# A mixing layer: the branch's part added on TensorE and ScalarE during the scaling turns, and six scaled additions a tile on VectorE instead of ten

## What is computed

```python
H_res = sinkhorn_log(x_norm @ W_res.T + base)         # 4x4 a row, 50 iterations
H_pre, H_post = softmax(x_norm @ W_pre.T + ..), softmax(x_norm @ W_post.T + ..)
H_res = (1 - g) * I + g * H_res
x_pre = einsum('btnc,btn->btc', x_streams, H_pre)
y = x_pre @ W_branch                                    # the branch
x_mixed = einsum('btij,btjc->btic', H_res, x_streams)
return x_mixed + einsum('btc,btn->btnc', y, H_post)
```

## Time and profile before

| | |
|---|---|
| time, median of 3 runs | 2952.16 us (2950.13 to 2953.05) |
| the profiled execution | 2949.29 us |
| its span | 2947.6 us |
| granted TensorE clock, mean | 0.94 of full speed |
| PE busy | 2588.3 us (88%), 15056 instructions |
| DVE busy | 1821.9 us (62%), 4485 instructions |
| ACT busy | 1082.8 us (37%), 2317 instructions |

### The profile page before, as it was taken

How to read it: one execution, slowest core, us unless ns; L and a number is a source line. 1 busy time by engine, 2 the same in 40 slices (tenths; PEclk the granted TensorE clock), 3 DMA queues, 4 the chain that set the end, 5 groups by cost and what they waited for, 6 DMA issues and landing times. The chain is left out here.

```text
span 2947.6 us, 50657 instructions
## 1 busy us (share of the span) xinstructions
PE 2588.3 (88%) x15056; PEld 1807.8 (61%) x15056; DVE 1821.9 (62%) x4485; ACT 1082.8 (37%) x2317; POOL 1123.7 (38%) x801
## 2 busy tenths in 40 slices
PE   7999997999998899553759999978999987996999
PEld 6665644765553688542647555536665644885887
DVE  5677775567774433788766766764677773215443
ACT  2345554154555211442511545542355554002000
POOL 7456553555664000000044655536456552002110
PEclk9999998999999899666979999989999998998999
DMA  4323312432320521000134322223232313434111
GB/s 163 102 84 84 95 49 68 147 92 66 102 69 30 180 71 43 0 0 7 80 128 135 86 83 85 79 73 110 77 96 78 103 42 138 141 121 150 65 64 44
DMA packets 121079, 252.95 MB, mean 86 GB/s; under 512 B 12720, under 2 KB 39728, under 8 KB 120880
## 3 DMA queue, kind: packets, MB, share of 16 engines
q1 hardware_dynamic: 120912, 251.03, 26.7%
HBM read 166.57 MB, written 84.41 MB: 85 GB/s over the span
## 5 line engine op out<-in xcount | busy, mean ns | idle before, releaser
L617 ACT ACTIVATE a_prob<-a_pst 128x512 f32<-128x512 f32 (+3 forms) x1536 | 660.9, 493 | 572.2 <-PE a_pst L898 566.4
L710 DVE CUSTOM_DVE_ANT_0 a_psh<-a_psh,a_edge 128x128 f32<-128x128 f32 (+3 forms) x1024 | 480.1, 516 | 198.0 <-PE a_psh L851 170.6
L851 PE MATMUL a_psh<-a_kst,a_qst 127*128 127x512 f32 (+3 forms) x1536 | 485.3, 364 | 26.3 <-DVE a_mx L710 14.4
L898 PE MATMUL a_pst<-a_qst,a_kst 128*128 128x512 f32 (+2 forms) x1536 | 487.2, 372 | 23.1 <-DMA a_qst<-rowmax 18.6
L517 POOL TENSOR_TENSOR a_prob<-a_prob 128x2048 f32<-128x2048 f32 (+1 forms) x96 | 405.6, 4225 | 242.5 <-PE a_ppv L914 242.5
L851 PEld LDWEIGHTS a_psh<-a_kst,a_qst 127*128 127x128 f32 x1536 | 272.4, 189 | 240.2 <-DVE a_mx L713 92.7
L713 DVE TENSOR_REDUCE a_mx<-a_psh 128x1 f32<-128x512 f32 x512 | 329.3, 685 | 127.3 <-PE a_psh L851 126.2
L898 PEld LDWEIGHTS a_pst<-a_qst,a_kst 128*128 128x128 f32 x1536 | 287.5, 194 | 163.9 <-ACT a_prob L617 103.5
L914 PE MATMUL a_ppv<-a_prob,a_vg 128*32 128x512 f32 (+3 forms) x3072 | 319.2, 502 | 0.0
L502 POOL TENSOR_SCALAR_AFFINE_SELECT a_prob<-a_prob 128x512 f32<-128x512 f32 x256 | 161.9, 639 | 188.1 <-ACT a_prob L617 187.9
L927 PE MATMUL a_pden<-a_prob,a_ones 128*32 128x512 f32 (+3 forms) x2304 | 220.1, 475 | 14.1 <-POOL a_prob L517 14.1
(11 more groups left out here) (227 smaller groups left out, 4164.1 us busy)
## 6 DMA issues: line engine op xcount, KB each, us to landing
a_qst<-q SPq DMA_DIRECT2D x192, 256.0 KB, 4.5
a_wraw<-in_wqkv SPq DMA_DIRECT2D x52, 512.0 KB, 4.3
q<-a_stg_hi SPq DMA_DIRECT2D x64, 256.0 KB, 2.1
q<-a_stg_lo SPq DMA_DIRECT2D x64, 256.0 KB, 2.4
a_kst<-kT SPq DMA_DIRECT2D x96, 128.0 KB, 2.6
oT<-a_oT SPq DMA_DIRECT2D x32, 256.0 KB, 2.4
oT<-a_vT SPq DMA_DIRECT2D x32, 256.0 KB, 2.9
h_oraw<-oT SPq DMA_DIRECT2D x16, 512.0 KB, 4.0
```

The costliest lines, as they stand in the source:

```text
L617: act.activation(prob[k % len(prob)][:, h, off:], pst[:, (k * GH + h) % 3, off:], ACT.Exp, scale=scale).then_inc(s["exp_done"], 1)
L710: part = dve.tensor_tensor_reduce(scores, scores, edge[:, BANK - n:], 1.0, 2 * MASKED, ALU.add, ALU.max, mx_hq[kc][:, h, qt:qt + 1])
L851: mm = pe.matmul(psh[:, at, i * n:(i + 1) * n], qst[par][0:P - 1, h, qt * P:(qt + 1) * P], kst[par][0:P - 1, kc * BANK:kc * BANK + n], sta ...
L898: pe.matmul(pst[:, (k * GH + h) % 3, off:], kst[par][:, ki * P:(ki + 1) * P], qst[par][:, h, qc * BANK + off:(qc + 1) * BANK], start=True, ...
```

## The change

Four things are altered, all within `mixing_layer`.

- In the scaling turns each tile gets its branch part: ScalarE writes four more diagonals with H_post (semaphore `dq`), TensorE forms in `h_pout` the sum of the identity times the old stream and the H_post diagonal times y, for all four streams (eight products, `add_branch`, semaphore `xy`), and ScalarE copies the 128x1024 result back over `h_x` (`copy_x`, semaphore `xc`). These run one turn late: turn t adds the branch of tile t-1.
- The normalised tile is written once, into `z_all`, four tiles at a time: tiles 0 to 3 ahead of the turns, then 4 to 7, 8 to 11 and 12 to 15 inside turns 1, 5 and 9, as a loop of ScalarE. y is kept in two small buffers.
- The turns are written out (`for t in range(NT)`), where they were a loop on the engine.
- In the last phase no product and no addition concerns y. TensorE makes streams 0 and 1 with four products each and half of stream 2 (its terms 0 and 1, in the PSUM buffer `h_pz`); ScalarE still writes ten diagonals a tile. VectorE makes stream 3 and the other half of stream 2 with six scaled additions, in groups of two, two, one and one with a drain between them, then adds `h_pout` as before, and `h_pz` in a second, 128x256 addition.

```diff
-    PR0, PT0, YR0, Y0, MI0 = 1, 1, 1, 1, 2
-    HALF = NS // 2
+    PR0, PT0, YR0, MI0 = 1, 1, 1, 2
+    ON_PE = [(i, n) for i in range(2) for n in range(NS)] + [(2, 0), (2, 1)]
+    ON_DVE = (((3, 0), (2, 2)), ((3, 1), (2, 3)), ((3, 2),), ((3, 3),))
+    NP = len(ON_PE)
...
-            with act.Fori(0, NT) as t:
-                act.wait_ge(s["pre_ready"], t + 1)
-                act.activation(z[0][:, :], tile(x, t), ACT.Identity, bias=nmr[:, ds(t, 1)],
-                               scale=rstd[:, ds(t, 1)]).then_inc(s["z2"], 1)
+            def normalised(first):
+                with act.Fori(first, first + 4) as t:
+                    act.activation(tile(z_all, t), tile(x, t), ACT.Identity, bias=nmr[:, ds(t, 1)],
+                                   scale=rstd[:, ds(t, 1)]).then_inc(s["z2"], 1)
+            def pre_diagonals(t):
                 for n in range(NS):
-                    act.activation(dg[0][:, n, :], ident[:, :], ACT.Copy, scale=pp[:, ds(t, 1), 0, n])\
+                    act.activation(dg[0][:, n, :], ident[:, :], ACT.Copy, scale=pp[:, t, 0, n:n + 1])\
                         .then_inc(s["dp"], 1)
-                act.activation(tile(z_all, t), tile(x, t), ACT.Identity, bias=nmr[:, ds(t, 1)],
-                               scale=rstd[:, ds(t, 1)])
+            def copy_x(t):
+                act.wait_ge(s["xy"], t + 1)
+                act.activation(x[:, t, :], pout[:, :, :].rearrange("p a n -> p (a n)"), ACT.Copy).then_inc(s["xc"], 1)
+            def branch(t):
                 act.wait_ge(s["pre_ready"], PR0 + t + 1)
                 act.wait_ge(s["y_ready"], t + 1)
                 act.activation(preT[:, :, :], ppre[:, 0:C].rearrange("p (k n) -> p k n", n=P), ACT.Copy)\
                     .then_inc(s["preT"], 1)
+                if t % 4 == 1 and t + 3 < NT:
+                    normalised(t + 3)
+                if t + 1 < NT:
+                    pre_diagonals(t + 1)
+                if t:
+                    copy_x(t - 1)
+                for n in range(NS):
+                    act.activation(dg[0][:, NS + n, :], ident[:, :], ACT.Copy, scale=pp[:, t, 1, n:n + 1])\
+                        .then_inc(s["dq"], 1)
                 act.wait_ge(s["y_ready"], YR0 + t + 1)
-                act.activation(tile(y_all, t), py[:, 0:C], ACT.Copy).then_inc(s["y"], 1)
+                act.activation(y[t % 2], py[:, 0:C], ACT.Copy).then_inc(s["y"], 1)
+            normalised(0)
+            pre_diagonals(0)
+            for t in range(NT):
+                branch(t)
+            copy_x(NT - 1)
...
-                    for i in range(HALF):
-                        for n in range(NS):
-                            act.activation(dg[par][:, i * (NS + 1) + n, :], ident[:, :], ACT.Copy,
-                                           scale=m[:, ds(t, 1), i * NS + n]).then_inc(s["dm"], 1)
-                        act.activation(dg[par][:, i * (NS + 1) + NS, :], ident[:, :], ACT.Copy,
-                                       scale=pp[:, ds(t, 1), 1, i]).then_inc(s["dm"], 1)
+                    for at, (i, n) in enumerate(ON_PE):
+                        act.activation(dg[par][:, at, :], ident[:, :], ACT.Copy,
+                                       scale=m[:, ds(t, 1), i * NS + n]).then_inc(s["dm"], 1)
...
-            dve.wait_ge(s["y"], Y0 + NT)
+            dve.wait_ge(s["xc"], NT)
             with dve.Fori(0, NT // 2) as j:
                 for par in range(2):
                     t = j * 2 + par
-                    for n in range(NS):
-                        zn = z_all[:, ds(t, 1), n * C:(n + 1) * C].rearrange("p o n -> p (o n)")
-                        for i in range(HALF, NS):
-                            dve.scalar_tensor_tensor(stream(t, i), zn, m[:, ds(t, 1), i * NS + n], stream(t, i),
-                                                     ALU.mult, ALU.add)
-                        dve.drain()
-                    for i in range(HALF, NS):
-                        dve.scalar_tensor_tensor(stream(t, i), tile(y_all, t), pp[:, ds(t, 1), 1, i], stream(t, i),
-                                                 ALU.mult, ALU.add)
+                    for at, terms in enumerate(ON_DVE):
+                        if at:
+                            dve.drain()
+                        for i, n in terms:
+                            dve.scalar_tensor_tensor(stream(x, t, i), stream(z_all, t, n), m[:, ds(t, 1), i * NS + n],
+                                                     stream(x, t, i), ALU.mult, ALU.add)
                     dve.wait_ge(s["mix"], MI0 + t + 1)
-                    cols = x[:, ds(t, 1), 0:HALF * C].rearrange("p o n -> p (o n)")
-                    dve.tensor_tensor(cols, cols, pout[:, par, 0:HALF * C], ALU.add)
+                    cols = x[:, ds(t, 1), 0:2 * C].rearrange("p o n -> p (o n)")
+                    dve.tensor_tensor(cols, cols, pout[:, par, :], ALU.add)
+                    dve.tensor_tensor(stream(x, t, 2), stream(x, t, 2), pz[:, par, 0:C], ALU.add)
...
+            def add_branch(t):
+                pe.wait_ge(s["y"], t + 1)
+                pe.wait_ge(s["dq"], NS * t + NS)
+                for n in range(NS):
+                    cols = pout[:, n // 2, n % 2 * C:n % 2 * C + C]
+                    pe.matmul(cols, ident[:, :], x[:, t, n * C:(n + 1) * C], start=True, stop=False, skip_group_check=True)
+                    mm = pe.matmul(cols, dg[0][:, NS + n, :], y[t % 2], start=False, stop=True,
+                                   skip_group_check=True)
+                mm.then_inc(s["xy"], 1)
+            def branch(t, first):
                 pe.wait_ge(s["z2"], t + 1)
                 pe.wait_ge(s["preT"], t + 1)
                 pe.wait_ge(s["dp"], NS * t + NS)
                 for c in range(C // P):
                     for n in range(NS):
-                        mm = pe.matmul(ppre[:, c * P:(c + 1) * P], z[0][:, n * C + c * P:n * C + (c + 1) * P],
+                        mm = pe.matmul(ppre[:, c * P:(c + 1) * P],
+                                       z_all[:, t, n * C + c * P:n * C + (c + 1) * P],
                                        dg[0][:, n, :], start=(n == 0), stop=(n == NS - 1))
                 mm.then_inc(s["pre_ready"], 1)
-                pe.wait_ge(s["y"], t + 1)
+                if t > 1:
+                    pe.wait_ge(s["xc"], t - 1)
+                if not first:
+                    add_branch(t - 1)
                 pe.wait_ge(s["preT"], PT0 + t + 1)
                 for k in range(C // P):
                     mm = pe.matmul(py[:, 0:C], preT[:, k, :], wb[:, k, :], start=(k == 0), stop=(k == C // P - 1))
                 mm.then_inc(s["y_ready"], 1)
-            pe.wait_ge(s["y"], Y0 + NT)
+            for t in range(NT):
+                branch(t, t == 0)
+            pe.wait_ge(s["xc"], NT - 1)
+            add_branch(NT - 1)
+            pe.wait_ge(s["xc"], NT)
             with pe.Fori(0, NT // 2) as j:
                 for par in range(2):
                     t = j * 2 + par
                     pe.wait_ge(s["mixed"], t + 1)
-                    for i in range(HALF):
-                        for n in range(NS + 1):
-                            if n == 0:
-                                pe.wait_ge(s["dm"], (t * HALF + i) * (NS + 1) + NS + 1)
-                            rhs = z_all[:, ds(t, 1), n * C:(n + 1) * C].rearrange("p o n -> p (o n)") if n < NS \
-                                else tile(y_all, t)
-                            mm = pe.matmul(pout[:, par, i * C:(i + 1) * C], dg[par][:, i * (NS + 1) + n, :], rhs,
-                                           start=(n == 0), stop=(n == NS), skip_group_check=True)
+                    for at, (i, n) in enumerate(ON_PE):
+                        if n == 0:
+                            pe.wait_ge(s["dm"], t * NP + min(at + NS, NP))
+                        out = pout[:, par, i * C:(i + 1) * C] if i < 2 else pz[:, par, 0:C]
+                        mm = pe.matmul(out, dg[par][:, at, :], stream(z_all, t, n), start=(n == 0),
+                                       stop=(i, n + 1) not in ON_PE, skip_group_check=True)
                     mm.then_inc(s["mix"], 1)
```

More of the change, by code:

```diff
@@ L1140, in mixing_layer @@
         "stats", "rstd", "rms_in", "rms", "z", "zT_ready", "zT", "logit", "read", "gate", "e_in", "e_out",
-        "pp", "z2", "dp", "pre_ready", "preT", "y_ready", "y", "h_res", "dm", "mix", "mixed", "stored")}
+        "pp", "z2", "dp", "pre_ready", "preT", "y_ready", "y", "dq", "xy", "xc", "h_res", "dm", "mix", "mixed", "stored")}
     w_loaded, o_loaded, x_loaded = [s[f"wl{k}"] for k in range(KC)], (s["ol0"], s["ol1"]), (s["x0"], s["x1"])
     M0, L0, S0, ZR0, ZT0, LG0, RD0, MX0, DMA0 = 4, 2, 2, 4, 2, 2, 2, 2, 16
-    PR0, PT0, YR0, Y0, MI0 = 1, 1, 1, 1, 2
-    HALF = NS // 2
+    PR0, PT0, YR0, MI0 = 1, 1, 1, 2
+    ON_PE = [(i, n) for i in range(2) for n in range(NS)] + [(2, 0), (2, 1)]
+    ON_DVE = (((3, 0), (2, 2)), ((3, 1), (2, 3)), ((3, 2),), ((3, 3),))
+    NP = len(ON_PE)
```

(15 more changed lines are left out.)

## The result

The changed kernel takes 2913.31 us, the median of four runs (2911.69 to 2916.31), against 2951.14 us before: a ratio of 0.9876 with a 95% interval of 0.9862 to 0.9891, or 37.8 us less. The forecast was 2928 with a range of 2923 to 2941. The direction was right, the size too small: 24 us were forecast. The profiled execution has a span of 2912.1 us, 35.5 less than the 2947.6 before.

What follows compares the result with a forecast made beforehand. Sinkhorn, the first tile, then VectorE's fifteen tiles were taken to bound the mixing layer; -0.29 (first tile) + 0.35 (second addition) - 15 x 1.61 = -24.1 us, so 2952.16 became 2928, range 2923 to 2941.

Steps and rivals of the forecast that it cites:

- What bounds the stage: Mixing layer: Sinkhorn on VectorE, the first tile on TensorE, then fifteen tiles on VectorE set its end; turns had 42 us spare.
- The tile: Last phase on VectorE: each tile 1.61 us shorter, from 6.42 to 4.81 us, over 15 tiles.
- The chain: Last phase, VectorE's scaled additions up to a tile's 128x512 addition: 3.21 us instead of 5.17, 1.96 less.
- the unseen addition: Last phase, VectorE's new 128x256 addition of `h_pz`, not in the old trace: 0.35 us a tile, between 0.26 and 0.60.
- over 5 was the sign: Last phase: if right, VectorE waits for TensorE in the first tile alone, now over 5 us.
- The first tile: Start of last phase: TensorE's first product waits for four diagonals instead of five, so it starts 0.29 us earlier.
- The turns: Scaling turns beside Sinkhorn: 8.2 us each at full clock, ending at 1356, 29 us before `h_res`, at no cost.
- the 3.79 of the `h_ppre` sums: Scaling turns on TensorE: the sums for `h_ppre` were put at 3.79 us at most within a turn.
- A: Scaling turns: TensorE stays at the lower clock, turns of 12.7 us outlast Sinkhorn, kernel 14 us slower, 2966; chance 0.06.
- B: Last phase: TensorE becomes the bound below clock 0.90; at 0.75 a tile takes 5.76, total 2942; chance 0.10.
- C: Scaling turns: turns of about 11 us end 12 us late and halve the gain, about 2946; chance 0.04.
- None of the three is late next: Last phase: TensorE, ScalarE's diagonals and the tile's store all keep up with 4.81 us a tile; TensorE is nearest.

## Why the prediction was wrong in size

- **What bounds the stage**: right. Sinkhorn, the first tile, then VectorE's tiles, before and after.
- **The tile**: right in mechanism, and 0.10 us a tile too long: forecast 4.81, measured 4.71. The chain was met (3.20 for 3.21) and the unseen addition too (0.33 for 0.35). The addition is 0.02 of it; most of the rest, 0.07, is the idle time between tiles, which I carried over: 0.37 and 0.79 in turn before, 0.38 and 0.63 now. The runs show that the second of these, at the loop's top, moves with the code (0.93 and 1.19 with only the branch moved). In all fifteen tiles give 25.7 and not 24.2 us. VectorE's wait in the first tile is 4.5 us, where over 5 was the sign.
- **The first tile**: -0.29 forecast, -1.1 measured. The 7.3 us of products were 6.4, because the clock rose sooner: from 1390 to 1393 it is 1.00, where the kernel before has 0.75 from 1391 to 1394. That is chance: the kernel before with drains that came later than this tile has 7.99, the unchanged kernel 8.95, the changed one 7.81 and 8.45 in its two runs.
- **The turns**: no cost, as forecast, but the size was off: 8.2 us a turn forecast, 6.3 measured, end at 1323.6 for 1356. The step that failed is the 3.79 of the `h_ppre` sums, taken from rows at the lower clock while the rest of the turn was priced at the full one. With 1.95 in its place the prediction's own sum gives 6.7 a turn, by ScalarE's way. The clock did rise: 0.90 in the stretch, 0.96 up to the turns' end. The cover is 60 us, and 55 us more work in it were free.
- **Rivals**: A was priced right (each us beyond Sinkhorn's end is paid in full) and did not occur; its ground, a clock that stays at the 0.70 of the old turns, is not there: the new turns have 0.96. The swing of the clock with short pauses that the Trainium skill describes ("TensorE: Matmul & The Clock Gate", section "A second HAM failure mode: psum-queue depth-cycling") does not show in them. They hardly test it, as TensorE works 104 of their 118.6 us. B did not occur: VectorE waited for TensorE once. C's doubt, what written-out code costs in the turns, came to nothing: neither ScalarE nor TensorE has an idle piece over 0.8 us in them without a releaser.
- **The step that made it wrong**: that the sum ends with the mixing layer. "None of the three is late next" spoke of this stage alone, and the later stages stand in the sum at nothing, without a reason given. Their code is the same, but its place is not: a pass of the last phase's loop holds 16 instructions fewer in VectorE's program (62 before, 46 now, counted in the traces), and behind the two jumps of the next stage's loop that saves 4.1 + 3.8 = 7.9 us. The stage as a whole is 9.4 us shorter; the other 1.5 are within what the same kernel varies by. Putting 16 instructions back makes the two stretches 7.8 us longer and the median 2923.8, just inside the range. The mixing layer itself gave 27.8 us for the 24.1 forecast: 1.5 in the fifteen tiles, 0.8 in the first and 1.5 ahead of Sinkhorn. The trace of before held the hint: two stages of the same code, 846.3 and 858.0 us from first to last scan.

What stays open: why the second load comes 4 us behind the first and not at once, and what moves the stage by some us away from the two jumps, in the changed kernel against itself too. The change also writes out loops of TensorE and ScalarE and so moves the later code of both; no run moved that back, and only what lies behind the two jumps is shown to come from VectorE's.

## What to carry to other kernels

Price a change also by the instructions that it takes out of or puts into an engine's program, since all later code on that engine moves with them, as VectorE's did here; when two stages run the same code, compare their lengths first, and if they differ, look for idle pieces named "issue" at the loop's top. Before a change is judged by a few us, a run with some do-nothing instructions in a spot where the engine is idle tells how much of the figure is the place of the code; look at the stretches where the pauses stand, as whole stages of one trace vary by some us. And work beside a long serial stretch on another engine is free up to its end and costs in full beyond it, so its duration has to be worked out at the clock that the new load itself brings about.

## What the runs showed of the hardware

- At jumps back to the top of the attention's loop VectorE stands idle for about 2 us (1.9 to 2.4 in all runs) with nothing to wait for, and goes on about 2 us after a load of 8192 bytes began on an instruction queue. Where the instructions lie 16 further on, in the kernel before and with 16 drains, there is one piece of about 6 us instead (6.14 and 5.75; 5.78 and 5.77). That the edge between two loads falls right behind the loop's top there is the explanation that fits, argued from the loads' times.
- 112 drains behind the last tile lengthen the layer's end by 2.2 us in the changed kernel and by 1.7 in the old one; 16 and 64 lengthen it by 1.2 each.
- Eight 32-bit products of 128 columns take 1.95 us at a granted clock of 1.00 and 3.79 at 0.50 (the sums of `h_ppre`).
- Work on TensorE and ScalarE beside Sinkhorn leaves VectorE's small operations nearly as they were: 179.2 us before, 179.8 with the most work beside them.
